# A five-stage network on one core: each stage's first row, its norm and its K and Q weights are prepared while the stage before runs its last row

## The chip, the cores and the metric

The kernel runs on 1 core of one Trainium2 chip. The metric is the device time of a run in microseconds. Everything is float32. The engines are PE (TensorE), DVE (VectorE), ACT (ScalarE), POOL (GpSimd) and SP (SyncE), which issues nearly all DMAs.

## The reference, cut to what matters

A batch of 8 rows `x[b]` of 512 tokens by 512 features goes through four layers; a "row" below is one b. The first two are linear attention: a layer norm, K, Q and V projections, a softmax of K over the tokens and of Q over the features of a head, the product of K and V, then Q times that. The third is ordinary softmax attention with 16 heads. Each of the three ends with a norm modulated by the condition `emb`, a SiLU, an output product and the residual. The fourth is a state-space layer in two directions. In the reference's terms:

```
h  = layernorm(x);  k, q, v = h @ Wk + bk, h @ Wq + bq, h @ Wv + bv
y  = attention(q, k, v, mask)
x  = x + silu(layernorm(y) * (1 + scale(emb)) + shift(emb)) @ W_out + b_out          # three times
xs = layernorm(x) * ada_scale(c) + ada_shift(c);  xn = layernorm(xs)
mx = silu(xn @ Wx.T + bx);  z = xn @ Wz.T + bz                                       # fourth layer
y  = sum over two directions of ssm(z @ Wc.T);  out = x + gate * ((y * mx) @ Wf.T + bf + xs)
```

## The kernel before, in words

`program` (L2230) runs six blocks one after the other, each closed by `sems.clear()` (L97), which frees the semaphores and ends in a barrier of all engines (L100): `prologue` (L103, modulation vectors and fused weights), `attention_layer` (L309 and on) for layer 0 and for layer 1, `softmax_layer` (layer 2), `front_layer` (the fourth layer's two norms and the products that don't depend on the scan) and `scan_layer` (the scan over time and the output). A block's SBUF tensors are its own and are given back at its end.

Within a block each engine has its own instruction list in the order in which the code issues it, and engines meet on semaphores. SP issues loads in the order written and waits in that order too.

In an attention layer a row b takes these steps: `norms(b)` on DVE (statistics L850, aggregation L854, then the normalised row `xn` L875) with the inverse root on POOL between them (L671, L673); PE transposes `xn` (stage "T", L491), ACT drains the transposes with the norm's weights into `xn_t` (L702); PE makes K (L500) and Q (L509). `norms(b + 1)` runs within row b, and so do T, K and Q of row b + 1; so only row 0 has them ahead of everything else. All engines wait for all the constants first (`const_loaded`, five DMAs). `x` has two buffers, `xn` one.

`softmax_layer` does the same with its own table: `slots` gives each step of a row (16 groups of four heads' scores) some "filler" parts of the rows around it (T, K, Q, V of the next row, YT, TY, O of the one before), which all share the bank `f_bank`. DVE's `maxima` (L1377) read the scores, ACT's exponentials and PE's transposes follow. Between them DVE has `norm_stats(b + 1)` in group 0, `normed(b + 1)` in group 1, `y_norm_stats` in group 3 and `y_normed` in group 5.

`front_layer` per row: two norms on DVE with POOL's inverse roots (statistics L1643, `xs` L1651, scale L1655, shift L1659, second statistics L1663, `xn` L1673), POOL's residual in three steps of a whole row (L1548, L1551, L1554), PE's transposes (L1590), the two small products with `w_dbc` (L1598, L1605), the 64 products with `wx` (L1615), ACT's drains. `scan_layer` begins with a product for the step size (L2017), the z product (L2035) and the fused matrices; from then on POOL's product of states (L1892) and DVE's scan (L2204) run all the time.

## Time and profile before

| | us |
|---|---|
| median of 3 runs | 5849.61 (5847.49 to 5851.81) |
| profiled execution | 5854.08 |
| its span, first to last instruction | 5852.3 |
| prologue, to the next block's first instruction | 200.8 |
| attention layer 0, attention layer 1 | 626.4, 614.1 |
| softmax layer | 1251.6 |
| front layer | 383.7 |
| scan layer | 2775.8 |

The stages are cut at each block's first POOL instruction, a memset right behind the barrier (200.81, 827.19, 1441.27, 2692.83 and 3076.54 us). The mean granted TensorE clock is 0.977 of full speed. In a timeline a line gives the start, the time from there to the end of the last of its instructions, the engine, the line of the code, the operation, the tile written and the tiles read, the count, and in brackets how long the engine had been idle and what released it. A tile's name has its block's prefix (`l_` for the attention and softmax layers, `fr_` for the front, `sc_` for the scan). SPq are DMA issues.

### The profile page before, as it was taken

The page shows a single profiled execution, that of the slowest core. Times are in us where ns is not written, and L with a number is a line of the kernel's source. Part 1 is how long each engine was busy: PE and PEld are TensorE (multiplying, and loading weights), DVE is VectorE, ACT ScalarE, POOL GpSimd, SP SyncE. Part 2 cuts the span into 40 slices and gives each one's busy share as a digit, 9 for nine tenths or more (in the row PEclk, how much of TensorE's full clock was granted, in tenths as well). Part 3 has the DMA queues.
Part 4 walks back from the last instruction along what each step waited for, and adds up shares of the span by engine and source line. Part 5 has one row for each costly group of instructions (what it writes and reads, how often), then busy time and mean ns, then how long its engine had stood idle before and what let it go on. Part 6 is the DMA issues. An engine that isn't in the chain of part 4 may idle for free. (4 is left out here: it accounts for less than half of the span.)

```text
span 5852.3 us, 136486 instructions
## 1 busy us (share of the span) xinstructions
PE 5457.4 (93%) x58510; PEld 3277.8 (56%) x58510; DVE 4269.2 (73%) x5872; ACT 2978.4 (51%) x4999; POOL 2908.6 (50%) x955
## 2 busy tenths in 40 slices
PE   8899979997898998985998999999999999999998
PEld 3455545554454555552444566666666666666665
DVE  1455535554355555565638999999999999999996
ACT  0122212221465555551116777777777777777774
POOL 0000000010000000002427999999999999999997
PEclk9999989998999999997999999999999999999999
DMA  6200020111000000002432111211111121111210
GB/s 230 73 33 32 24 77 17 36 36 49 26 1 17 17 17 17 17 8 111 155 115 84 54 62 58 67 49 46 54 60 65 58 69 54 45 49 60 65 58 32
DMA packets 145195, 321.73 MB, mean 55 GB/s; under 512 B 25945, under 2 KB 27226, under 8 KB 134378
## 3 DMA queue, kind: packets, MB, share of 16 engines
q1 hardware_dynamic: 142322, 309.20, 15.3%
q8 instruction: 448, 7.34, 0.5%
q10 hardware_dynamic: 2304, 4.20, 0.2%
q14 instruction: 121, 0.99, 0.1%
HBM read 238.46 MB, written 74.89 MB: 54 GB/s over the span
## 5 line engine op out<-in xcount | busy, mean ns | idle before, releaser
L1892 POOL TENSOR_TENSOR sc_state<-sc_state,sc_c_rows 128x2048 f32<-128x2048 f32 x512 | 2331.4, 4568 | 124.0 <-DVE sc_state L2204 123.0
L2204 DVE TENSOR_TENSOR_SCAN sc_state<-sc_decay,wide 128x512 f32<-128x512 f32 x2048 | 2335.3, 1198 | 28.0 <-PE wide L2062 20.9
L2062 PEld LDWEIGHTS wide<-sc_diag,sc_du_t 64*64 64x64 f32 x32768 | 1048.0, 133 | 526.6 <-issue 343.9
L2062 PE MATMUL wide<-sc_diag,sc_du_t 64*64 64x128 f32 x32768 | 1218.7, 272 | 19.9 <-DVE sc_state L2204 19.6
L2078 PE MATMUL wide<-sc_state,sc_half 64*64 64x512 f32 x8192 | 1199.1, 592 | 7.5 <-POOL sc_state L1892 7.0
L1996 ACT ACTIVATE sc_decay<-sc_delta,sc_neg_a 128x512 f32<-128x512 f32 x1024 | 723.6, 719 | 448.8 <-DVE sc_state L2204 443.9
L1996 ACT ACTIVATE sc_decay<-sc_delta_x,sc_neg_a 128x512 f32<-128x512 f32 x1024 | 710.0, 717 | 286.8 <-DVE sc_state L2204 282.6
L1377 DVE CUSTOM_DVE_ANT_0 l_prob<-wide,l_mask_add 128x512 f32<-128x512 f32 x512 | 340.0, 683 | 286.9 <-PE wide L1247 286.7
L2078 PEld LDWEIGHTS wide<-sc_state,sc_half 64*64 64x64 f32 x8192 | 405.6, 133 | 168.4 <-issue 127.1
L1162 ACT ACTIVATE l_prob<-l_prob,l_s_max 128x512 f32<-128x512 f32 x512 | 366.0, 716 | 229.3 <-DVE l_s_max L1377 228.9
L2035 PE MATMUL wide<-sc_xn_t,sc_w_z 128*128 128x512 f32 x1024 | 477.0, 609 | 1.7 <-DMA sc_xn_t<-xn_d 1.7
L509 PE MATMUL wide<-l_w,l_xn_t 128*128 128x512 f32 x1024 | 445.1, 592 | 1.7 <-PEq L84 1.7
L1258 PE MATMUL wide<-l_ident,l_prob 128*128 128x128 f32 x2048 | 293.2, 280 | 65.7 <-DVE l_prob_t L1386 38.5
L1258 PEld LDWEIGHTS wide<-l_ident,l_prob 128*128 128x128 f32 x2048 | 225.3, 142 | 222.5 <-issue 134.7
L1119 POOL TENSOR_TENSOR l_out<-l_x,l_rows 128x2048 f32<-128x2048 f32 x8 | 36.3, 4532 | 605.9 <-DMA x<-l_out 599.8
L509 PEld LDWEIGHTS wide<-l_w,l_xn_t 128*128 128x128 f32 x1024 | 193.1, 190 | 241.2 <-issue 241.2
L671 POOL TENSOR_SCALAR l_rstd<-l_mv 128x4 f32<-128x4 f32 x16 | 3.8, 236 | 647.5 <-DVE l_mv L854 647.5
L2035 PEld LDWEIGHTS wide<-sc_xn_t,sc_w_z 128*128 128x128 f32 x1024 | 185.3, 191 | 211.0 <-issue 211.0
L1226 PE MATMUL wide<-l_xn_t,l_w 128*128 128x512 f32 x512 | 251.0, 636 | 25.3 <-ACT l_h_t L1153 19.0
L2090 PE MATMUL wide<-sc_w_out,sc_y_sum 128*128 128x256 f32 x1024 | 244.3, 383 | 6.6 <-DVE sc_o_gated L2191 3.6
L500 PE MATMUL wide<-l_xn_t,l_w 128*128 128x512 f32 x512 | 226.2, 600 | 24.6 <-ACT l_xn_t L702 22.8
L509 PE MATMUL wide<-l_w,l_h_t 128*128 128x512 f32 x512 | 226.5, 601 | 1.7 <-ACT l_h_t L702 1.7
(203 smaller groups left out, 6669.5 us busy)
## 6 DMA issues: line engine op xcount, KB each, us to landing
sc_c_rows<-c_d SPq DMA_DIRECT2D x64, 1024.0 KB, 4.8
sc_w_z<-wz_tiles SPq DMA_DIRECT2D x128, 256.0 KB, 2.7
x<-l_out SPq DMA_DIRECT2D x24, 1024.0 KB, 4.2
l_x<-x SPq DMA_DIRECT2D x16, 1024.0 KB, 6.1
mx_d<-fr_mx SPq DMA_DIRECT2D x16, 1024.0 KB
sc_mx<-mx_d SPq DMA_DIRECT2D x64, 256.0 KB, 2.8
pro_w_mod<-in_mod_w SPq DMA_DIRECT2D x6, 2048.0 KB, 10.9
l_w<-in_att_w SPq DMA_DIRECT2D x12, 1024.0 KB, 12.5
```

The lines of the kernel that those rows point to most:

```text
L509: last = pe.matmul(bank_of(name, t)[:, :], src_t[:, k, t * P:(t + 1) * P], weight[:, k, :], start=(k == 0), stop=(k == DT - 1))
L1162: act.activation(prob[:, u % (2 * HG), :], prob[:, u % (2 * HG), :], ACT.Exp, scale=-1.0, bias=s_max[:, u % (2 * HG):u % (2 * HG) + 1], ac ...
L1226: last = pe.matmul(f_bank, weight[:, i, k * P:(k + 1) * P], xn_t[:, i, :], start=(i == 0), stop=(i == DT - 1))
L1258: last = pe.transpose(t_banks[u % 2][:, m * P:(m + 1) * P], prob[:, u % (2 * HG), m * P:(m + 1) * P], ident[:, :])
L1377: dve.tensor_tensor_reduce(out=prob[:, u % (2 * HG), :], in0=s_banks[i], in1=mask_add[b % 2][:, :], op0=ALU.add, op1=ALU.min, scale=-1.0, ...
L1892: pool.tensor_tensor(state[quad % STATES][:, :, :], state[quad % STATES][:, :, :], c_rows[(r * 4 + q) % ROWS][:, :, :], ALU.mult).then_inc ...
L1996: act.activation(decay[step % DECAYS][:, :], of[:, :], ACT.Exp, scale=neg_a[:, s, m, n:n + 1]).then_inc(decay_ready, 1)
L2035: last = pe.matmul(z_bank, w_z[slot % WZ][:, k, :], xn_t[:, k, :], start=(k == 0), stop=(k == DT - 1))
L2062: last = pe.matmul(to[cols_to, k, :, :], du_t[slot % 2][rows, k, of * 64:(of + 1) * 64], diag[r % 2][rows, c, k, :, :], start=True, stop=True)
L2078: ins = pe.matmul(acc[i][to * 64:(to + 1) * 64, :], half[g * 64:(g + 1) * 64, :], state[quad % STATES][g * 64:(g + 1) * 64, n, :], start=( ...
L2090: last = pe.matmul(z_bank[:, 0:256], y_sum[b % 2][:, k, t * P:(t + 1) * P], w_out[:, k, h * 256:(h + 1) * 256], start=(k == ks[0]), stop=( ...
L2204: dve.tensor_tensor_scan(state[quad % STATES][:, step % 4, order], decay[step % DECAYS][:, order], pair[:, i, order], 0.0, ALU.mult, ALU.a ...
```

## The change

The row buffer `x`, the norm's output `xn`, `ident` and the four weights get buffers that live across the blocks (`ahead`); the scaled row `xs` is shared from the attention layers on. In the prologue two of the three `w_mod` buffers lie over them, so the loads of row 0 and of layer 0's K and Q weights come behind the last product that reads those buffers. Every block then loads the following block's row 0 and, for the attention layers, its K and Q weights while its own last rows run, and makes the norm of that row on DVE and POOL. For the front layer, the softmax layer's last row makes both norms in six pieces, in groups 0, 1, 2, 4, 6 and 9. A block that starts counts those semaphores up instead (`sem_inc`). The wait for all constants at the head of PE and ACT goes: ACT waits for the columns alone (`cols_loaded`), which come first in SP's queue. In the front layer `w_dbc` and `wx` are loaded ahead of the ada rows and the other constants, PE waits for `w_dbc` where it uses it, and POOL's list starts with row 0's residual. In the scan layer four constants are issued on ACT's queue in place of SP's.

```diff
+                sp.wait_ge(piece_full, 4 * PIECES)
+                sp.dma_start(x[:, :, :], d["x"][0].rearrange("(t p) n -> p t n", p=P)).then_inc(x_loaded, 16)
+                for i in (1, 0):
+                    sp.dma_start(w_qk[i][:, :, :], d["att_w"][0, i].rearrange("(k p) n -> p k n", p=P)
+                                 ).then_inc(w_qk_loaded, 16)
...
@@ -363,7 +381,19 @@
...
+                dve.wait_ge(x_loaded, 16)
+                for t in range(TT):
+                    dve.bn_stats(stats[:, t, :], x[:, t, :]).then_inc(stats_ready, 1)
+                for t in range(TT):
+                    dve.wait_ge(stats_ready, t + 1)
+                    dve.bn_aggr(mv[:, t, :], stats[:, t, :]).then_inc(mv_ready, 1)
                 for j in range(2 * DT):
+                    if j == 3:
+                        dve.wait_ge(rstd_ready, 1)
+                    if 3 <= j < 3 + TT:
+                        t = j - 3
+                        dve.tensor_scalar(xn[:, t, :], x[:, t, :], mv[:, t, 0:1], rstd[:, t:t + 1],
+                                          ALU.subtract, ALU.mult)
                     dve.wait_ge(dbc_full, j + 1)
...
                     sp.sem_inc(x_stored[j], 16)
-                sp.dma_start(cols[:, :], d["att_cols"][:, layer, :]).then_inc(const_loaded, 16)
+                sp.dma_start(cols[:, :], d["att_cols"][:, layer, :]).then_inc(cols_loaded, 16)
+                sp.sem_inc(x_loaded[0], 16)
+                sp.dma_start(mask_in[0][:, :], d[f"mask{layer}"][0].broadcast_to([P, T])).then_inc(mask_loaded[0], 16)
...
-                load(0, 0)
-                for i in (1, 0, 2, 3):
+                for i in (0, 1):
+                    sp.sem_inc(w_ready[i], 16)
+                for i in (2, 3):
                     sp.dma_start(w[i][:, :, :], d["att_w"][layer, i].rearrange("(k p) n -> p k n", p=P)
                                  ).then_inc(w_ready[i], 16)
...
+                sp.wait_ge(xb_ready, B - 1)
+                sp.wait_ge(x_stored[0], 32)
+                sp.dma_start(x[0][:, :, :], x_out[0].rearrange("(t p) n -> p t n", p=P)).then_inc(x_loaded[0], 16)
+                for i, name in ((1, "K"), (0, "Q")):
+                    sp.wait_ge(psum_full, st.full(B - 2, name, 3))
+                    sp.dma_start(w[i][:, :, :], d["att_w"][layer + 1, i].rearrange("(k p) n -> p k n", p=P)
+                                 ).then_inc(w_ready[i], 16)
                 for j in range(2):
                     body(B - 2 + j, B // 2 - 1, j, False)
+                for i in range(2):
+                    sp.wait_ge(w_ready[i], 32)
...
                 def body(b, pair, j, last):
+                    norms(b + 1)
                     if not last:
-                        norms(b + 1, pair + j, 1 - j)
+                        residual(b + 1, pair + j, 1 - j)
...
-                act.wait_ge(const_loaded, 5 * 16)
+                act.wait_ge(cols_loaded, 16)
...
-                pe.wait_ge(const_loaded, 5 * 16)
...
-                dve.wait_ge(const_loaded, 5 * 16)
+                dve.sem_inc(stats_ready, TT)
+                dve.sem_inc(mv_ready, TT)
+                dve.sem_inc(xn_ready, TT)
+                dve.wait_ge(cols_loaded, 16)
+                dve.wait_ge(const_loaded, 3 * 16)
...
@@ -903,8 +949,9 @@
                 def body(b, pair, j, last):
                     if not linear:
                         mask(b, pair, j)
-                    if not last:
-                        norms(b + 1, pair + j, 1 - j)
+                    elif not last:
+                        mask(b + 1, pair + j, 1 - j)
+                    norms(b + 1, pair + j, 1 - j)
...
-                norms(0, 0, 0)
...
-                sp.dma_start(cols[:, :], d["att_cols"][:, layer, :]).then_inc(const_loaded, 16)
+                sp.dma_start(cols[:, :], d["att_cols"][:, layer, :]).then_inc(cols_loaded, 16)
+                sp.sem_inc(x_loaded, 16)
+                for i in range(2):
+                    sp.sem_inc(w_ready[i], 16)
+                sp.dma_start(w[2][:, :, :], d["att_w"][layer, 2].rearrange("(k p) n -> p k n", p=P)
+                             ).then_inc(w_ready[2], 16)
...
-                load(0)
                 load_mask(0)
-                for i in (1, 0, 2):
-                    sp.dma_start(w[i][:, :, :], d["att_w"][layer, i].rearrange("(k p) n -> p k n", p=P)
-                                 ).then_inc(w_ready[i], 16)
...
+                    if b == B - 2:
+                        sp.wait_ge(xb_ready, B)
+                        sp.wait_ge(x_stored[0], 16)
+                        sp.dma_start(x[:, :, :], x_out[0].rearrange("(t p) n -> p t n", p=P)).then_inc(x_loaded, 16)
+                        sp.dma_start(ada[:, :, :].rearrange("p r n -> p (r n)"),
+                                     d["ada_d"][0:1, 0:2 * D].broadcast_to([P, 2 * D])).then_inc(ada_loaded, 16)
...
                 for b in range(B):
-                    norms(b)
+                    if b >= 1:
+                        norms(b)
                     if b >= 2:
                         y_norms(b - 2)
                     biased(b)
+                norms(B)
                 y_norms(B - 2)
+                norms(B + 1)
...
+                def front_normed():
+                    dve.wait_ge(rstd_ready, B + 1)
+                    for t in range(TT):
+                        dve.tensor_scalar(xs[:, t, :], x[:, t, :], mv[:, t, 0:1], rstd[:, t:t + 1],
+                                          ALU.subtract, ALU.mult).then_inc(xs_normed, 1)
+
+                def front_scaled():
+                    dve.wait_ge(ada_loaded, 16)
+                    for t in range(TT):
+                        dve.wait_ge(xs_normed, t + 1)
+                        dve.tensor_tensor(xs[:, t, :], xs[:, t, :], ada[:, 0, :], ALU.mult).then_inc(xs_scaled, 1)
+
+                def front_shifted():
+                    for t in range(TT):
+                        dve.wait_ge(xs_scaled, t + 1)
+                        dve.tensor_tensor(xs[:, t, :], xs[:, t, :], ada[:, 1, :], ALU.add).then_inc(xs_ready, 1)
+
+                def front_stats():
+                    dve.wait_ge(rstd_ready, B + 1)
+                    for t in range(TT):
+                        dve.wait_ge(xs_ready, t + 1)
+                        dve.bn_stats(stats[:, t, :], xs[:, t, :]).then_inc(stats_ready, 1)
+                    for t in range(TT):
+                        dve.wait_ge(stats_ready, (B + 1) * TT + t + 1)
+                        dve.bn_aggr(mv[:, t, :], stats[:, t, :]).then_inc(mv_ready, 1)
+
+                def front_xn():
+                    dve.wait_ge(rstd_ready, B + 2)
+                    dve.wait_ge(f_full, full("T", B - 1, DT - 1))
+                    for t in range(TT):
+                        dve.tensor_scalar(xn[:, t, :], xs[:, t, :], mv[:, t, 0:1], rstd[:, t:t + 1],
+                                          ALU.subtract, ALU.mult)
...
-                    if g == 0 and b + 1 < B:
+                    if g == 0:
                         norm_stats(b + 1)
                     if g == 1 and b + 1 < B:
                         normed(b + 1)
+                    if b == B - 1:
+                        if g == 1:
+                            front_normed()
+                        if g == 2:
+                            front_scaled()
+                        if g == 4:
+                            front_shifted()
+                        if g == 6:
+                            front_stats()
+                        if g == 9:
+                            front_xn()
...
-                    sp.dma_start(x[b % 2][:, :, :], x_in[b].rearrange("(t p) n -> p t n", p=P)
-                                 ).then_inc(x_loaded[b % 2], 16)
+                    if b >= 1:
+                        sp.dma_start(x[b % 2][:, :, :], x_in[b].rearrange("(t p) n -> p t n", p=P)
+                                     ).then_inc(x_loaded[b % 2], 16)
                     sp.dma_start(ada[b % 2][:, :, :].rearrange("p r n -> p (r n)"),
                                  d["ada_d"][b:b + 1, :].broadcast_to([P, 3 * D])).then_inc(ada_loaded[b % 2], 16)
 
+                sp.sem_inc(x_loaded[0], 16)
+                sp.dma_start(w_dbc[:, :, :, :].rearrange("p s k n -> p (s k n)"), d["wdbc_d"]).then_inc(w_dbc_loaded, 16)
+                sp.dma_start(wx[:, :, :], d["wxT"].rearrange("(k p) n -> p k n", p=P)).then_inc(wx_loaded, 16)
                 load(0)
-                sp.dma_start(ident[:, :], d["ident"]).then_inc(const_loaded, 16)
                 sp.dma_start(b_bias[:, :, :].rearrange("p s n -> p (s n)"), d["dbc_bias_d"].broadcast_to([P, 192])
                              ).then_inc(const_loaded, 16)
                 for s in range(2):
...
                     if b == 0:
-                        pool.wait_ge(const_loaded, 6 * 16)
+                        pool.wait_ge(const_loaded, 4 * 16)
+                        pool.wait_ge(ada_loaded[0], 16)
...
-                for b in range(B):
+                for done in (var_ready, rstd_ready, var2_ready, rstd2_ready):
+                    pool.sem_inc(done, 1)
+                residual(0)
+                for b in range(1, B):
                     rsqrt(b, mv, rstd, mv_ready, var_ready, rstd_ready)
                     rsqrt(b, mv2, rstd2, mv2_ready, var2_ready, rstd2_ready)
                     residual(b)
...
-                act.wait_ge(const_loaded, 6 * 16)
...
-                pe.wait_ge(const_loaded, 6 * 16)
...
                     pe.wait_ge(t_drained, (b + 1) * DT)
+                    if b == 0:
+                        pe.wait_ge(w_dbc_loaded, 16)
...
+                for done in (stats_ready, mv_ready, norm_ready, scale_ready, xs_ready, stats2_ready, mv2_ready, xn_ready):
+                    dve.sem_inc(done, TT)
+                for b in range(1, B):
...
-                sp.dma_start(ident[:, :], d["ident"]).then_inc(const_loaded, 16)
...
             @block.scalar
             def _(act):
+                act.dma_start(wdt[:, :, :, :].rearrange("p s i n -> p (s i n)"), d["wdt"]).then_inc(const_loaded, 16)
+                act.dma_start(neg_a[:, :, :, :].rearrange("p s k n -> p (s k n)"), d["alog"]).then_inc(const_loaded, 16)
+                act.dma_start(ident[:, :], d["ident"]).then_inc(const_loaded, 16)
+                act.dma_start(half[:, :], d["half_ident"]).then_inc(const_loaded, 16)
...
+        with ExitStack() as shared:
+            held = lambda n, s: shared.enter_context(nc.sbuf_tensor("ahead_" + n, s, F32))
+            pairs = [held("xn_wq", [P, ET, 512]), held("x_wk", [P, ET, 512])]
+            ahead = {"ident": held("ident", [P, P]), "xn": pairs[0][:, 0:TT, :], "x": pairs[1][:, 0:TT, :],
+                     "w": [p[:, TT:ET, :] for p in pairs], "w_mod": pairs}
+            prologue(nc, sems, d, mod_all, banks, ahead)
+            sems.clear()
+            ahead["w"] += [held("w2", [P, DT, D]), held("w3", [P, DT, D])]
+            ahead["xs"] = held("xs", [P, TT, D])
```

The first place where instructions move is DVE in the softmax layer's last row, at group 2. `l_prob` are the scores with the mask, `l_prob_t` the transposed probabilities, `l_y` the rescaled attention output of the row before. Before:

```order
L1386 COPY l_prob_t<-wide 128x512
L1377 ISA l_prob,l_s_max<-wide,l_mask_add 128x512
L1377 ISA l_s_max 128x1
L1352 TENSOR_TENSOR l_y<-wide,l_q_sum 128x512 x2
L1377 ISA l_prob,l_s_max<-wide,l_mask_add 128x512
L1377 ISA l_s_max 128x1
```

And after the change, where `ahead_xs` is the front layer's scaled row:

```order
L1478 COPY l_prob_t<-wide 128x512
L1469 ISA l_prob,l_s_max<-wide,l_mask_add 128x512
L1469 ISA l_s_max 128x1
L1444 TENSOR_TENSOR l_y<-wide,l_q_sum 128x512
L1397 TENSOR_TENSOR ahead_xs<-ahead_xs,l_ada 128x512 x4
L1444 TENSOR_TENSOR l_y<-wide,l_q_sum 128x512
L1469 ISA l_prob,l_s_max<-wide,l_mask_add 128x512
```

A multiplication of four instructions now stands between the two drains of `l_y`; five other pieces stand in groups 0, 1, 4, 6 and 9.

The second is POOL's list at the start of the front layer, up to row 1's second inverse root (`fr_rstd`), before:

```order
L1532 MEMSET fr_minus_half 128x4
L1537 TENSOR_SCALAR fr_rstd<-fr_mv 128x4
L1539 TENSOR_TENSOR fr_rstd<-fr_rstd,fr_minus_half 128x4
L1537 TENSOR_SCALAR fr_rstd<-fr_mv 128x4
L1539 TENSOR_TENSOR fr_rstd<-fr_rstd,fr_minus_half 128x4
L1548 TENSOR_TENSOR fr_resid<-fr_xs,fr_bf_row 128x2048
L1551 TENSOR_TENSOR fr_resid<-fr_resid,fr_ada 128x2048
L1554 TENSOR_TENSOR fr_resid<-fr_resid,fr_x 128x2048
L1537 TENSOR_SCALAR fr_rstd<-fr_mv 128x4
```

And after:

```order
L1634 MEMSET fr_minus_half 128x4
L1651 TENSOR_TENSOR fr_resid<-ahead_xs,fr_bf_row 128x2048
L1654 TENSOR_TENSOR fr_resid<-fr_resid,fr_ada 128x2048
L1657 TENSOR_TENSOR fr_resid<-fr_resid,ahead_x_wk 128x2048
L1639 TENSOR_SCALAR fr_rstd<-fr_mv 128x4
L1641 TENSOR_TENSOR fr_rstd<-fr_rstd,fr_minus_half 128x4
L1639 TENSOR_SCALAR fr_rstd<-fr_mv 128x4
L1641 TENSOR_TENSOR fr_rstd<-fr_rstd,fr_minus_half 128x4
```

Row 0's two inverse roots are gone from it, and the three steps of row 0's residual stand ahead of row 1's inverse roots.

The third is SP's list at the same place, before:

```order
L1487 DMA fr_x<-x 128x4x512
L1489 DMA fr_ada<-ada_d 128x1536
L1493 DMA fr_ident<-in_ident 128x128
L1494 DMA fr_b_bias<-dbc_bias_d 128x192
L1497 DMA fr_c_bias<-dbc_bias_d 80x1 x2
L1499 DMA fr_bf_row<-in_bf_row 128x512
L1500 DMA fr_w_dbc<-wdbc_d 128x768
L1502 DMA fr_wx<-in_wxT 128x4x1024
L1487 DMA fr_x<-x 128x4x512
```

And after:

```order
L1596 DMA fr_w_dbc<-wdbc_d 128x768
L1597 DMA fr_wx<-in_wxT 128x4x1024
L1592 DMA fr_ada<-ada_d 128x1536
L1599 DMA fr_b_bias<-dbc_bias_d 128x192
L1602 DMA fr_c_bias<-dbc_bias_d 80x1 x2
L1604 DMA fr_bf_row<-in_bf_row 128x512
L1590 DMA fr_x<-x 128x4x512
L1592 DMA fr_ada<-ada_d 128x1536
```

The two weights went to the head, row 0 is no longer loaded, and row 1 and its ada rows stay behind the small constants.

## Rows read from the trace of the kernel before

**Rows 1.** Page, part 1: busy us, share, instructions of PE.

```profile
PE 5457.4 (93%) x58510; PEld 3277.8 (56%) x58510; DVE 4269.2 (73%) x5872; ACT 2978.4 (51%) x4999; POOL 2908.6 (50%) x955
```

**Rows 2.** Timeline, first attention start: start, us, engine, line, op, tiles, count, [idle, releaser].

```profile
200.81 0.10 POOL L663 MEMSET l_minus_half<- 128x4 f32 x1 [197.35 <-POOLq L100]
...
206.40 0.18 DVE L842 TENSOR_SCALAR l_keep<-l_keep_in 128x32 f32<-128x32 int32 x1 [7.80 <-DMA l_keep_in<-in_mask_t]
...
218.86 3.34 ACT L702 ACTIVATE l_xn_t<-wide,l_cols 128x512 f32<-128x512 f32 x4 [43.84 <-PE wide L491]
...
222.25 14.00 PE L500 MATMUL wide<-l_xn_t,l_w 128*128 128x512 f32 x32 [0.87 <-ACTq L84]
```

**Rows 3.** Timeline, second attention start.

```profile
827.19 0.10 POOL L663 MEMSET l_minus_half<- 128x4 f32 x1 [29.33 <-POOLq L100]
...
848.40 16.24 PE L500 MATMUL wide<-l_xn_t,l_w 128*128 128x512 f32 x32 [0.87 <-ACTq L84]
```

**Rows 4.** Timeline, softmax stage start.

```profile
1441.27 0.10 POOL L1105 MEMSET l_minus_half<- 128x4 f32 x1 [28.66 <-POOLq L100]
...
1461.22 0.78 ACT L1147 ACTIVATE l_xn_t<-wide,l_cols 128x512 f32<-128x512 f32 x1 [1.21 <-PE wide L1215]
...
1466.03 6.03 PE L1226 MATMUL wide<-l_xn_t,l_w 128*128 128x512 f32 x8 [0.87 <-ACT l_xn_t L1147]
```

**Rows 5.** DMA issues: tiles, kind, count, KB, median us to landing.

```profile
ssm_cols<-in_ssm_cols SPq DMA_DIRECT2D x1, 36.0 KB, 1.8
```

**Rows 6.** Timelines of POOL, DVE and PE, front stage, first two rows.

```profile
2692.83 0.10 POOL L1532 MEMSET fr_minus_half<- 128x4 f32 x1 [35.77 <-POOLq L100]
...
2715.45 4.49 POOL L1548 TENSOR_TENSOR fr_resid<-fr_xs,fr_bf_row 128x2048 f32<-128x2048 f32 x1
...
2700.34 2.47 DVE L1643 BATCH_NORM_STATS2 fr_stats<-fr_x 128x6 f32<-128x512 f32 x4 [12.80 <-DMA fr_ada<-ada_d]
...
2715.51 14.44 DVE L1673 TENSOR_SCALAR fr_xn<-fr_xs,fr_mv,fr_rstd 128x512 f32<-128x512 f32 x4 [1.47 <-POOL fr_rstd L1539]
...
2734.08 1.91 DVE L1651 TENSOR_SCALAR fr_xs<-fr_x,fr_mv,fr_rstd 128x512 f32<-128x512 f32 x4 [1.47 <-POOL fr_rstd L1539]
...
2745.65 13.78 DVE L1673 TENSOR_SCALAR fr_xn<-fr_xs,fr_mv,fr_rstd 128x512 f32<-128x512 f32 x4
...
2734.82 7.09 PE L1598 MATMUL wide<-fr_xn_t,fr_w_dbc 128*80 128x512 f32 x16 [0.87 <-ACT fr_xn_t L1570]
...
2772.79 1.04 PE L1590 MATMUL wide<-fr_ident,fr_xn 128*128 128x128 f32 x8
```

**Rows 7.** Timeline of DVE, softmax stage, rows 6 and 7 of eight.

```profile
2391.67 0.69 DVE L1377 CUSTOM_DVE_ANT_0 l_prob<-wide,l_mask_add 128x512 f32<-128x512 f32 x1 [0.25 <-PE wide L1247]
...
2395.31 2.47 DVE L1315 BATCH_NORM_STATS2 l_stats<-l_x 128x6 f32<-128x512 f32 x4
...
2398.55 0.68 DVE L1377 CUSTOM_DVE_ANT_0 l_prob<-wide,l_mask_add 128x512 f32<-128x512 f32 x1
...
2405.21 0.68 DVE L1377 CUSTOM_DVE_ANT_0 l_prob<-wide,l_mask_add 128x512 f32<-128x512 f32 x1
...
2539.98 0.69 DVE L1377 CUSTOM_DVE_ANT_0 l_prob<-wide,l_mask_add 128x512 f32<-128x512 f32 x1 [0.25 <-PE wide L1247]
...
2544.96 0.69 DVE L1377 CUSTOM_DVE_ANT_0 l_prob<-wide,l_mask_add 128x512 f32<-128x512 f32 x1 [0.65 <-PE wide L1247]
...
2551.09 0.69 DVE L1377 CUSTOM_DVE_ANT_0 l_prob<-wide,l_mask_add 128x512 f32<-128x512 f32 x1 [0.36 <-PE wide L1247]
```

**Rows 8.** Timeline, scan stage start.

```profile
3078.35 0.48 SPq L1756 DMA_DIRECT2D sc_dlt<-dlt_d  x1
...
3087.25 6.07 PE L2035 MATMUL wide<-sc_xn_t,sc_w_z 128*128 128x512 f32 x8 [1.68 <-DMA sc_xn_t<-xn_d]
```

**Rows 9.** Timeline, first attention layer, last row.

```profile
768.61 0.18 DVE L910 RECIPROCAL l_k_sum<-l_k_sum 128x4 f32<-128x4 f32 x1
...
781.30 1.91 PE L491 MATMUL wide<-l_ident,l_k_t 128*128 128x128 f32 x16
```

106 lines of the change are left out of this document (56 added, 50 removed).

## The prediction

> **What bounds the kernel now.** I read the page's busy times first, then timelines around each of the five places where one stage ends and the next begins, then the softmax stage's last two rows of the batch. PE is busy for 93% of the span [rows 1], so little is to be had inside the stages; the reader is to look at their starts. There PE stands idle. R below is the moment when a stage's first POOL instruction, a memset, runs, right behind the barrier.
>
> In the first attention stage R is 200.81 and the first K product starts at 222.25, which is R + 21.4. Between them the constants land (DVE L842 at 206.40 is released by the last of them), then row 0, then its norm runs, then the transposes and ACT's four drains of 3.34 us [rows 2]. In the second it is 848.40 - 827.19 = 21.2 [rows 3], in the softmax stage 1466.03 - 1441.27 = 24.8 [rows 4]. The front stage is the dearest: its first product is at 2734.82, R + 42.0, because row 0 goes through two norms and because DVE's last normalisation takes 14.44 us beside POOL's residual, which starts at the same moment (2715.45 against 2715.51) [rows 6]. The scan stage starts its z product when xn_t has landed [rows 8].
>
> **Part by part.** (1) Attention starts. Loading row 0, its statistics, rsqrt and normalisation leave the start; K and Q weights are there already. PE's first 16 transposes can run at once, since PE waits for no constant any more. What is late next is ACT's first drain, which needs the column constants, the first DMA of SP. A transfer of like kind landed 1.8 us after its issue [rows 5], so with the issue at R + 0.1 ACT drains from R + 2.2, needs its 3.34 us [rows 2], and K starts at R + 5.6. Gain 21.4 - 5.6 = 15.8 and 21.2 - 5.6 = 15.6. DVE still waits for all constants (R + 5.6 before [rows 2]) and the mask, but K's first group comes only some 3.5 us after K starts (a fourth of 14.00 [rows 2]), at R + 9, so this wait is covered; if the mask came after that, each us would cost one. Bounds: if ACT's constants came only when all five did before, R + 5.6, K would start at R + 9.0 and each gain be 3.4 smaller; the other end is the clock.
>
> (2) The clock. In the second stage the first matmuls ran at the lower level, 1.2 GHz: 32 products took 16.24 us, against 14.00 in the first stage [rows 2, 3], so a start at the lower level costs 2.2. The second stage keeps its cost. The first one ran its K at full clock after the transposes; I allow 0.5 there for a later rise, and take 15.3; the ends are 0 and 2.2. The Trainium skill (TensorE: Matmul & The Clock Gate, section "What's actually happening") says that the throttled state is the default and activity releases it; by that every start, the first one too, pays the full amount, and the first gain would be 13.6 instead of 15.3.
>
> (3) Softmax start. Its transposes go through a single bank: each step is a drain of 0.78 and a wait of 1.21 [rows 4]. With the first drain at R + 2.3 the fourth ends at R + 2.3 + 3 x 1.99 + 0.78 = R + 9.05, and K follows at R + 9.1. Gain 24.8 - 9.1 = 15.7; its first 8 products keep their 6.03 us. Bounds 12.3 (constants late by 3.4) and 17.9 (clock up in time).
>
> (4) Front start. PE starts its transposes at R + 0.2 and w_dbc is now SP's first load, so row 0's products start at about R + 5 instead of R + 42. By that alone the gain would be 37. But row 1 is late next. Before, DVE had row 1's xn ready long before PE asked (DVE's 13.78 us from 2745.65 end at 2759.4, PE's transposes start at 2772.79 [rows 6]). Now POOL has row 0's residual in its queue ahead of row 1's rsqrt, and it waits for the constants and the ada rows. These stand behind 2.5 MB of weights in SP's queue: about 3.6 MB in all. Before, 1.8 MB were in at R + 7.5 (DVE L1643 at 2700.34 [rows 6]); with 2 us before the first byte that is 0.33 MB per us, so I estimate 2 + 3.6 / 0.33 = R + 13. POOL's three steps at 4.49 end at R + 26.5; rsqrt and its hand-over take 1.5; DVE starts xs of row 1 at R + 28, comes to xn 11.6 later (2734.08 to 2745.65) at R + 39.6, and needs 13.8 there beside POOL's next residual: R + 53.4. PE, going from R + 5 by the old distance of 38.0 (2734.82 to 2772.79), asks at R + 43. It stalls for 10.4 us. Row 1's transposes come at R + 53.4 instead of R + 80.0: gain 26.6, less 1 which I allow for matmuls at the lower clock after that stall, 25.7. Row 2 has time to spare again, because a DVE row (about 30 us: 2.8 of statistics, 1.5, 11.6 and 13.8) is shorter than PE's 42. Bounds: 37 without the stall, 22 if POOL starts 4 us later still.
>
> (5) Scan start. Four DMA issues ahead of SP's other loads go to ACT's queue, about 0.45 us each by their neighbour [rows 8], so at most 1.8. The z product waits for xn_t, whose bytes still share the engines with these constants; I take 1.3, between 0 and 2.5. The Trainium skill (DMA: Bandwidth & Descriptors, section "Queues, rings and completion order") says that a DMA engine takes turns between queues packet by packet; by that the constants no longer stand ahead of xn_t but beside it, the same bytes come first, and the gain would be near 0 instead of 1.3.
>
> (6) What is added. Where a last row runs, DVE now does the next stage's row. In the two attention stages that is a norm of about 6.5 us right behind 768.61, which every other row has too; k_t is then ready at about 777, and PE asks for it at 781.30 [rows 9]. Covered, cost 0; without the cover 6.5 each. In the prologue DVE mostly waits for PE; 0. The softmax stage's last row is not free: DVE's new blocks stand between the maxima that PE's scores wait for. How dear such a block is, rows 6 and 7 tell. With the statistics (2.47 and 0.36) the step from 2391.67 to 2398.55 takes 6.88, the same step without them 4.98 (2539.98 to 2544.96): 1.90. With the normalisation of 1.9 us the next one takes 6.66 against 6.13: 0.53 [rows 7]. The last row gets six blocks: statistics 1.9, normalisation 0.5, scale 1.35, shift 1.65 (each 2.4 us long, so between the two), second statistics 1.5, second normalisation 0.1 to 0.3 beside output products. Together 7.0 lost. Bounds: 4 (all at the cheaper price per us of block) and 14 (all six exposed).
>
> **Sum.** 15.3 + 15.6 + 15.7 + 25.7 + 1.3 - 7.0 = 66.6 us. The profiled execution took 5854.1 (span 5852.3), so 5787.5 by its own measure; it lies 4.5 above the median of the runs, 5849.6, and for a median I forecast 5783.
>
> **Rivals.** A: the front stall doesn't come, since DVE's xn slips between POOL's steps or POOL starts early. The order of the rows is against it: POOL and DVE started together and DVE lost 12.5 us [rows 6]. Then 10.4 + 1 us more: 5772. B: the starts stay bound by constants, at R + 5.6 as before, in all three attention-like stages, and w_dbc comes late by 2: 3 x 3.4 = 10.2 less, 5793. For it: SP issues one DMA after another; against it: the columns are first. C, slower than before: POOL's long instructions hold DVE's normalisations wherever they are put. There are 20 added or moved ones (4 in the prologue, 4 in each attention stage, 8 in the softmax stage). One held takes (14.44 - 0.5) / 3 = 4.6 instead of about 0.5 [rows 6], 4.1 more; 20 x 4.1 = 82, and with nothing of it covered the sum turns to 15 slower, 5865. It decides from 17 of 20 held. Against it: POOL is idle in those last rows. D: the change doesn't bring the work forward, because a preload lands late and DVE, which runs in order, stops in front of it with the maxima behind it. The start's gain of one stage (15) is then spent where it was won, twice over if both: 5799 to 5815.
>
> **Chances.** The forecast 0.66, A 0.12, B 0.12, D 0.06, C 0.04. All bounds together at the good end give 15.8 + 17.8 + 17.9 + 37 + 2.5 - 4 = 87, at the bad end 11.9 + 12.2 + 12.3 + 22 + 0 - 14 = 44, so 5763 to 5805. They won't all fall one way; 5769 to 5800 holds A and B and leaves about 2 in 10 out. A measurement of this kernel can tell about 0.2%, 12 us, from no change: faster 0.94, within it 0.02, slower 0.04.
>
> **What would show it.** Right: K products at R + 5 to 6 in the attention stages and R + 9 in the softmax stage; PE idle for 8 to 12 us ahead of row 1's transposes in the front stage, with POOL's residual ahead of row 1's rsqrt; the last softmax row longer by 5 to 9 us. Wrong: K waits that end with a DMA of constants, a DVE wait for a preload in a last row, normalisations of 4.7 us in last rows, or a longer scan stage.

## The result and the profile after

| | before | after |
|---|---|---|
| median of the runs, us | 5850.71 (5847.49 to 5852.04, 4 runs) | 5797.5 (5793.07 to 5798.61, 4 runs) |
| ratio to the kernel before | | 0.9908 (95%: 0.9891 to 0.9926) |
| profiled execution, its span | 5854.08, 5852.3 | 5797.34, 5795.2 |
| prologue | 200.8 | 199.3 |
| attention layer 0, attention layer 1 | 626.4, 614.1 | 617.4, 602.0 |
| softmax layer | 1251.6 | 1237.7 |
| front layer | 383.7 | 362.6 |
| scan layer | 2775.8 | 2776.2 |

The kernel is 53 us faster, where 66.6 were forecast (5783); the time lies near the upper end of the range given (5769 to 5800). Between the two profiled executions the spans differ by 57.1: 1.5 + 9.0 + 12.1 + 13.9 + 21.1 - 0.5, block by block. These are two single executions, and a block of the same code differs by 2 to 7 us from one profile to the next; the table in "Why the prediction came out as it did" has the spread. R, the moment of a block's first POOL memset, is 199.34, 816.72, 1418.70, 2656.37 and 3018.99 now. The line of part 1 of the page that answers to [rows 1] has the same work in a shorter span:

```profile
PE 5459.9 (94%) x58510; PEld 3280.3 (57%) x58510; DVE 4264.0 (74%) x5872; ACT 2978.3 (51%) x4999; POOL 2907.3 (50%) x956
```

The start of the first attention layer after the change, a timeline (against [rows 2]):

```profile
199.34 0.10 POOL L703 MEMSET l_minus_half<- 128x4 f32 x1 [20.48 <-POOLq L100]
...
207.11 0.18 DVE L890 TENSOR_SCALAR l_keep<-l_keep_in 128x32 f32<-128x32 int32 x1 [10.12 <-DMA l_keep_in<-in_mask_t]
207.34 4.53 POOL L722 TENSOR_TENSOR l_out<-ahead_x_wk,l_rows 128x2048 f32<-128x2048 f32 x1 [7.91 <-DMA l_keep_in<-in_mask_t]
207.44 4.71 DVE L908 TENSOR_SCALAR l_mask_add<-l_mask_in 128x512 f32<-128x512 int32 x1
207.50 3.65 PE L520 MATMUL wide<-ahead_ident,ahead_xn_wq 128*128 128x128 f32 x16 [10.89 <-DVEq L84]
208.62 3.34 ACT L747 ACTIVATE l_xn_t<-wide,l_cols 128x512 f32<-128x512 f32 x4 [33.58 <-PE wide L520]
212.01 15.95 PE L529 MATMUL wide<-l_xn_t,ahead_x_wk 128*128 128x512 f32 x32 [0.87 <-ACTq L84]
```

The row at 207.50 is the one to look at. Row 0's `xn` had been finished at 191.1, PE waited for no constant in its own list, and yet its transposes start at R + 8.2. The bracket says what released them: DVE's sequencer at L84, a semaphore count, right behind the instruction at 207.11 that a DMA of constants released. L84 is `absent`: each engine counts up the drains that row 0 doesn't have, and PE's first transposes wait for DVE's count. It stands behind DVE's wait for the constants, as it did before, where `xn` came later anyway. K starts at R + 12.7, not R + 5.6. The second attention layer (against [rows 3]) shows the same, with K at R + 11.4:

```profile
823.73 3.50 PE L520 MATMUL wide<-ahead_ident,ahead_xn_wq 128*128 128x128 f32 x16 [13.29 <-DVEq L84]
...
828.10 14.00 PE L529 MATMUL wide<-l_xn_t,ahead_x_wk 128*128 128x512 f32 x32 [0.87 <-ACTq L84]
```

The softmax layer counts nothing of the kind, and its start (against [rows 4]) went as forecast, K at R + 8.5:

```profile
1420.43 0.78 ACT L1204 ACTIVATE l_xn_t<-wide,l_cols 128x512 f32<-128x512 f32 x1 [23.92 <-DMA l_cols<-in_att_cols]
...
1427.22 5.61 PE L1282 MATMUL wide<-l_xn_t,ahead_x_wk 128*128 128x512 f32 x8 [0.87 <-ACT l_xn_t L1204]
```

The front layer's first two rows after the change, timelines of POOL, DVE and PE (against [rows 6]):

```profile
2671.61 4.51 POOL L1651 TENSOR_TENSOR fr_resid<-ahead_xs,fr_bf_row 128x2048 f32<-128x2048 f32 x1 [15.13 <-DMA fr_bf_row<-in_bf_row]
...
2697.46 4.51 POOL L1651 TENSOR_TENSOR fr_resid<-fr_xs,fr_bf_row 128x2048 f32<-128x2048 f32 x1
...
2676.97 2.47 DVE L1751 BATCH_NORM_STATS2 fr_stats<-fr_x 128x6 f32<-128x512 f32 x4 [25.93 <-DMA fr_ada<-ada_d]
...
2686.66 1.91 DVE L1759 TENSOR_SCALAR fr_xs<-fr_x,fr_mv,fr_rstd 128x512 f32<-128x512 f32 x4 [6.95 <-POOL fr_rstd L1641]
...
2697.52 14.46 DVE L1781 TENSOR_SCALAR fr_xn<-fr_xs,fr_mv,fr_rstd 128x512 f32<-128x512 f32 x4
...
2661.94 9.46 PE L1704 MATMUL wide<-fr_xn_t,fr_w_dbc 128*80 128x512 f32 x16 [0.87 <-ACT fr_xn_t L1675]
...
2712.03 3.96 PE L1694 MATMUL wide<-ahead_ident,fr_xn 128*128 128x128 f32 x16 [9.60 <-DVE fr_xn L1781]
...
2716.86 9.30 PE L1704 MATMUL wide<-fr_xn_t,fr_w_dbc 128*80 128x512 f32 x16 [0.87 <-ACT fr_xn_t L1675]
```

This is the stall that the prediction worked out: POOL's residual of row 0 waits for the constants, row 1's inverse root waits for the residual, row 1's `xn` then takes 14.46 us beside the next residual, and PE stands for 9.60 us ahead of row 1's transposes. These come at R + 55.7 instead of R + 80.0.

In the softmax layer's last row (against [rows 7]) DVE's maxima of groups 1, 2 and 3 start here; between them stand the statistics and the two normalisations:

```profile
2496.59 0.69 DVE L1469 CUSTOM_DVE_ANT_0 l_prob<-wide,l_mask_add 128x512 f32<-128x512 f32 x1 [0.25 <-PE wide L1303]
...
2500.23 2.47 DVE L1374 BATCH_NORM_STATS2 l_stats<-ahead_x_wk 128x6 f32<-128x512 f32 x4
...
2503.47 0.68 DVE L1469 CUSTOM_DVE_ANT_0 l_prob<-wide,l_mask_add 128x512 f32<-128x512 f32 x1
...
2507.71 1.90 DVE L1390 TENSOR_SCALAR ahead_xs<-ahead_x_wk,l_mv,l_rstd 128x512 f32<-128x512 f32 x4
...
2510.13 0.68 DVE L1469 CUSTOM_DVE_ANT_0 l_prob<-wide,l_mask_add 128x512 f32<-128x512 f32 x1
```

The first step is 6.88 us (4.98 before, [rows 7]), the second 6.66 (6.13 before). Each maxima row that starts a group gives one such step. Against the same steps before, the six blocks cost 1.90, 0.53, 1.11 (scale), 1.67 (shift), 1.33 (second statistics) and 0.24 (`xn`): 6.8. The first five repeat within 0.02 us in the five other profiles of this code; the last doesn't (that step takes 8.16 to 8.88 us in them, against 8.55 before), so 0.24 is inside the spread. The normalisations in all the last rows took 1.90 to 1.92 us for four, so POOL held none of them.

In the last row of the first attention layer (against [rows 9]) DVE's norm stands ahead of the same reciprocal, `k_t` is ready at 768.4, and PE asks for it at 772.98. It cost nothing: from the last K product's start to the end of the layer it is 100.5 us, against 102.7 before (102.2 to 102.3 in four of the five other profiles of the same code, 100.5 in one), and in the second attention layer 102.1 us before and after.

```profile
764.66 1.92 DVE L921 TENSOR_SCALAR ahead_xn_wq<-ahead_x_wk,l_mv,l_rstd 128x512 f32<-128x512 f32 x4 [1.58 <-POOL l_rstd L715]
766.49 0.17 DVE L957 RECIPROCAL l_k_sum<-l_k_sum 128x4 f32<-128x4 f32 x1
...
772.98 1.91 PE L520 MATMUL wide<-ahead_ident,l_k_t 128*128 128x128 f32 x16
```

### The profile page after: what moved, and what is told of

Read it like the earlier page. It is cut to its first block and busy times, and to the rows that moved or that the text cites. A ratio compares the mean times of both kernels' runs of the same rounds, so it can differ in the third digit from the quotient of the medians.

```text
span 5795.2 us, 136527 instructions
## 1 busy us (share of the span) xinstructions
PE 5459.9 (94%) x58510; PEld 3280.3 (57%) x58510; DVE 4264.0 (74%) x5872; ACT 2978.3 (51%) x4999; POOL 2907.3 (50%) x956
## 3 DMA queue, kind: packets, MB, share of 16 engines
q10 hardware_dynamic: 2880, 4.95, 0.2%
## 5 line engine op out<-in xcount | busy, mean ns | idle before, releaser
L1314 PE MATMUL wide<-ahead_ident,l_prob 128*128 128x128 f32 x2048 | 294.1, 281 | 66.8 <-DVE l_prob_t L1478 39.2
L1314 PEld LDWEIGHTS wide<-ahead_ident,l_prob 128*128 128x128 f32 x2048 | 227.3, 143 | 224.0 <-issue 133.8
L1173 POOL TENSOR_TENSOR l_out<-ahead_x_wk,l_rows 128x2048 f32<-128x2048 f32 x8 | 36.3, 4535 | 610.1 <-DMA x<-l_out 598.4
L529 PE MATMUL wide<-l_xn_t,ahead_x_wk 128*128 128x512 f32 x512 | 225.9, 599 | 24.6 <-ACT l_xn_t L747 22.8
L747 ACT ACTIVATE l_k_tm<-wide 128x512 f32<-128x512 f32 x64 | 33.1, 607 | 379.4 <-PE wide L520 379.4
L1721 PE MATMUL wide<-fr_xn_t,fr_wx 128*128 128x512 f32 x512 | 226.8, 604 | 0.0
L538 PE MATMUL wide<-ahead_w,l_h_t 128*128 128x512 f32 x512 | 224.4, 597 | 1.7 <-ACT l_h_t L747 1.7
L538 PE MATMUL wide<-ahead_w,l_xn_t 128*128 128x512 f32 x512 | 222.5, 593 | 1.0 <-PEq L84 1.0
```

The lines of the kernel that those rows point to most:

```text
L538: last = pe.matmul(bank_of(name, t)[:, :], src_t[:, k, t * P:(t + 1) * P], weight[:, k, :], start=(k == 0), stop=(k == DT - 1))
L1314: last = pe.transpose(t_banks[u % 2][:, m * P:(m + 1) * P], prob[:, u % (2 * HG), m * P:(m + 1) * P], ident[:, :])
L1721: last = pe.matmul(banks[6 + m % 2], wx[:, k, m * P:(m + 1) * P], xn_t[j][:, k, :], start=(k == 0), stop=(k == DT - 1))
```

## The experiments

In each, times are medians against the kernel before on the same chip, with its ratio and 95% interval. The block lengths are from the profiled execution. The changed kernel's ratio, 0.9908, has the interval 0.9891 to 0.9926, and most of the intervals below overlap it. So what one edit did is read from the timelines, and the medians only agree with it; of the edited versions of the changed kernel, the last one alone is clear of it by its interval.

### DVE's count ahead of its waits

```diff
                 dve.sem_inc(xn_ready, TT)
+                first = [i[0] for i in plan].index("T")
+                absent(st, dve, drained["dve"], "dve", -1, plan[0][0], first)
                 dve.wait_ge(cols_loaded, 16)
...
-                first = [i[0] for i in plan].index("T")
-                absent(st, dve, drained["dve"], "dve", -1, plan[0][0], first)
```

> The changed kernel with one edit in both attention stages: DVE counts its absent parts up before it waits for the constants, not behind. In the changed kernel PE's transposes of row 0 started at R + 8.2 and R + 7.0, released by that count, and K at R + 12.7 and R + 11.4. My theory (PE waits for DVE's count, which stands behind the constants): the transposes start at R + 0.3, K at about R + 5.6 in both, 7.1 and 5.8 us earlier; K at the lower clock may take back 2 in the second. Time 5785 to 5788 against 5797.5 of the changed kernel, ratio to the kernel before 0.989. Rival (the transposes or ACT's drains are late by the DMAs themselves): K stays between R + 10 and R + 13, time 5796 to 5799, ratio 0.991.

Measured: 5782.26 us, ratio 0.9885 (0.9869 to 0.9902). The attention layers last 611.8 and 595.9 us instead of 617.4 and 602.0. Their start in PE's and ACT's timelines, with R at 201.12:

```profile
201.69 3.65 PE L520 MATMUL wide<-ahead_ident,ahead_xn_wq 128*128 128x128 f32 x16 [3.29 <-DVEq L84]
206.20 16.21 PE L529 MATMUL wide<-l_xn_t,ahead_x_wk 128*128 128x512 f32 x32 [0.87 <-ACTq L84]
...
202.92 3.23 ACT L747 ACTIVATE l_xn_t<-wide,l_cols 128x512 f32<-128x512 f32 x4 [26.08 <-DMA l_cols<-in_att_cols]
```

The transposes start at R + 0.6 and K at R + 5.1 (R + 5.5 in the second layer); ACT's first drain is at R + 1.8, released by the column constants, as the prediction had it. So the step was right in all but the one count that it overlooked. K runs at the lower clock in both layers (16.21 and 15.60 us for 32 products). The two blocks together are 11.7 us shorter than in the changed kernel's own profile, in which the second K ran at the higher clock. Against the five other profiles of the same attention code they are 13.4 to 16.1 us shorter, and the medians differ by 15.2.

### PE's own wait put back

```diff
             def _(pe):
+                pe.wait_ge(cols_loaded, 16)
+                pe.wait_ge(const_loaded, 3 * 16)
```

> The changed kernel, with PE in the two attention stages waiting again for the columns and the three other constants before anything else. My theory (PE is held by DVE's count, which comes behind the same constants, so its own wait was worth nothing): K at R + 12.7 and R + 11.4 within 0.3, time 5797.5 within 2, ratio 0.991. Rival (dropping PE's own wait is what gave the gain at the starts): K 3 to 6 us later in each, time 5803 to 5809, ratio 0.992 to 0.993.

Measured: 5795.29 us, ratio 0.9907 (0.989 to 0.9923), beside 0.9908 of the changed kernel. K at R + 12.8 and R + 11.7. The two layers last 619.7 and 604.1 us, which is 2.3 and 2.1 more than in the changed kernel's profile, but the same as in the fifth and sixth experiment (619.7 and 604.1; 619.4 and 604.1), which leave these layers alone. PE's wait could be given back at no cost, since DVE's count held it just as long: in the changed kernel its removal was worth nothing.

### The residual behind `xn`

```diff
                     pool.wait_ge(xs_ready, (b + 1) * TT)
+                    pool.wait_ge(xn_ready, (b + 1) * TT)
```

> The changed kernel, with POOL's residual of every front row waiting also until DVE has written that row's xn. In the changed kernel row 1's xn took 14.46 us beside the residual and PE stood 9.6 us before row 1's transposes (R + 55.7), with a lower clock behind it. My theory (the two hold each other): xn of row 1 takes about 1.9 us and ends near R + 43, PE starts the transposes at R + 46 without a stall, 9.6 us earlier, and 0 to 2.8 of clock come back. Time 5785 to 5788, ratio 0.989. Rival (the later residual delays the loads and xs of the rows behind): PE stalls by 5 us or more before row 2 or 3, time 5793 to 5800.

Measured: 5783.57 us, ratio 0.9883 (0.9867 to 0.99), the front layer 349.6 us instead of 362.6. Timelines of DVE and PE, with R at 2659.21:

```profile
2700.27 1.91 DVE L1782 TENSOR_SCALAR fr_xn<-fr_xs,fr_mv,fr_rstd 128x512 f32<-128x512 f32 x4
...
2705.09 1.04 PE L1695 MATMUL wide<-ahead_ident,fr_xn 128*128 128x128 f32 x8
```

The same four instructions take 1.91 us instead of 14.46, and the transposes start at R + 45.9 without a wait. The rows behind are not late: DVE's `xs` of row 2 starts at R + 58.1, in the changed kernel at R + 59.7. Three other profiles have the changed kernel's front code (first, second and sixth experiment): there row 1's transposes come at R + 54.8 to R + 54.9 and the block lasts 359.4 to 359.5 us. Against these the gain is 9.0 at the transposes and 9.8 in the block.

### Row 1's inverse roots ahead of the residual

```diff
-                residual(0)
                 for b in range(1, B):
                     rsqrt(b, mv, rstd, mv_ready, var_ready, rstd_ready)
                     rsqrt(b, mv2, rstd2, mv2_ready, var2_ready, rstd2_ready)
+                    if b == 1:
+                        residual(0)
                     residual(b)
```

> The changed kernel, with row 1's two inverse roots ahead of row 0's residual in POOL's list. By my prediction's step (row 1 is late because its inverse root stands behind the residual in POOL's queue) DVE's xs of row 1 starts at R + 25 instead of R + 30.3, its xn at about R + 36, and since POOL then starts row 0's residual at the same moment, xn still takes 14.4 us: transposes of row 1 at R + 50.2 instead of R + 55.7, stall 4 us instead of 9.6, time 5791 to 5794, perhaps 1 to 3 worse by a late row 2 because two residuals follow each other. Rival (POOL's order is not what sets row 1, the late load is): xs of row 1 stays at R + 30, time 5797.

Measured: 5792.25 us, ratio 0.9902 (0.9886 to 0.9919), the front layer 356.3 us. Timelines of POOL and PE, with R at 2656.99:

```profile
2679.50 0.24 POOL L1639 TENSOR_SCALAR fr_rstd<-fr_mv 128x4 f32<-128x4 f32 x1 [22.41 <-DVE fr_mv L1755]
...
2691.70 4.52 POOL L1651 TENSOR_TENSOR fr_resid<-ahead_xs,fr_bf_row 128x2048 f32<-128x2048 f32 x1
...
2706.31 1.10 PE L1695 MATMUL wide<-ahead_ident,fr_xn 128*128 128x128 f32 x8 [3.27 <-DVE fr_xn L1782]
```

`xs` of row 1 starts at R + 23.9 and the transposes at R + 49.3, with a wait of 3.3 us. POOL's order was worth 6.3 us (5.5 to 5.6 against the three other profiles); the rest is the collision, which this order keeps (`xn` 14.49 us).

### `wx` behind row 1

```diff
                 sp.dma_start(w_dbc[:, :, :, :].rearrange("p s k n -> p (s k n)"), d["wdbc_d"]).then_inc(w_dbc_loaded, 16)
-                sp.dma_start(wx[:, :, :], d["wxT"].rearrange("(k p) n -> p k n", p=P)).then_inc(wx_loaded, 16)
                 load(0)
...
                 load(1)
+                sp.dma_start(wx[:, :, :], d["wxT"].rearrange("(k p) n -> p k n", p=P)).then_inc(wx_loaded, 16)
```

> The changed kernel, with the 2 MB of wx behind row 1 and its ada rows in SP's queue of the front stage, not ahead of them. In the changed kernel POOL's residual of row 0 started at R + 15.2, DVE's statistics of row 1 at R + 20.6, xs at R + 30.3 and PE's transposes of row 1 at R + 55.7. My prediction's step (the weights ahead hold up the constants, and with them the residual and row 1): residual at R + 9, xs of row 1 at R + 24, its xn at R + 35 and still 14.4 us long beside the next residual, transposes at R + 49.5, 6 us earlier; the wx products wait up to 2 us for wx. Time 5790 to 5793. Rival (the constants land when they do because of their own small transfers, not the weights): residual at R + 14 or later, transposes at R + 54 or later, time 5796 to 5799.

Measured: 5783.76 us, ratio 0.9888 (0.9873 to 0.9903), the front layer 352.7 us. POOL's and DVE's timelines, with R at 2655.39:

```profile
2664.00 4.50 POOL L1651 TENSOR_TENSOR fr_resid<-ahead_xs,fr_bf_row 128x2048 f32<-128x2048 f32 x1 [8.51 <-DMA fr_bf_row<-in_bf_row]
...
2668.53 2.47 DVE L1751 BATCH_NORM_STATS2 fr_stats<-fr_x 128x6 f32<-128x512 f32 x4 [18.49 <-DMA fr_ada<-ada_d]
```

The residual starts at R + 8.6 instead of R + 15.2 and the transposes of row 1 at R + 49.1 instead of R + 55.7: 6.6 us (5.8 to 5.9 against the three other profiles). The 2 MB ahead were the reason. The block gains 9.9, because row 1's `w_dbc` products ran at full clock (7.09 us instead of 9.30); against the three other profiles, where they did too, it gains 6.7. The median is lower than forecast; its softmax layer lasted 1230.7 us, 7 less than in the changed kernel, at an edit that doesn't touch it.

### The front's row 0 in the tail of the softmax layer

```diff
-                    if g == 0:
+                    if g == 0 and b + 1 < B:
                         norm_stats(b + 1)
...
-                    if b == B - 1:
-                        if g == 1:
-                            front_normed()
...
                 y_normed(B - 1)
+                norm_stats(B)
+                front_normed()
+                front_scaled()
+                front_shifted()
+                front_stats()
                 for k in range(4):
                     drain("O", B - 1, k)
+                    if k == 0:
+                        front_xn()
...
-                norms(B)
                 y_norms(B - 2)
-                norms(B + 1)
                 y_norms(B - 1)
+                norms(B)
+                norms(B + 1)
```

> The changed kernel, with DVE's six blocks for the front layer's row 0 moved from the groups of the softmax stage's last row to its tail, behind the last normalised y and between the output drains, where DVE stood idle for 14.6 us and then 3.8 us at a time. In the changed kernel the stretch from the last K product's start to the end of that stage was 275.1 us against 267.9 before, at the same time of low clock (37.5 and 37.7 us). My theory (the blocks stand between the maxima that PE's scores wait for, and cost 7): 267.9 within 1 at a like clock, time 5789 to 5792. Rival (the 7 us come from something else in that row, or the tail pays them back): 274 to 276, time 5796 to 5799.

Measured: 5790.74 us, ratio 0.9898 (0.9882 to 0.9913). The stretch from the last K product's start to the block's end, as windows (length; PE, PEld, DVE, ACT, POOL busy; granted clock; DMA share; GB/s), first in the kernel before, then in the changed kernel, then in this one:

```profile
2424.97:2692.83 267.86, 220.14 (x1764) 124.17 (x1760) 135.57 (x323) 139.73 (x297) 7.08 (x5) 0.93 0.03 13
```

```profile
2381.30:2656.37 275.07, 221.45 (x1764) 125.00 (x1760) 148.47 (x355) 139.74 (x297) 9.58 (x9) 0.93 0.05 18
```

```profile
2386.00:2652.51 266.51, 217.29 (x1764) 122.63 (x1760) 149.41 (x355) 139.66 (x297) 9.59 (x10) 0.95 0.05 19
```

At the same clock the change made it 7.2 longer, with DVE's 32 instructions more; here DVE has them too, and the stretch is 266.5 at a slightly higher clock (27.3 us at the lower level instead of 37.4, which is worth some of it). The first six steps between the maxima behind group 1 are those of before (4.98, 6.13, 6.13, 6.31, 4.95, 5.47). DVE's timeline shows where the blocks went:

```profile
2618.43 2.46 DVE L1374 BATCH_NORM_STATS2 l_stats<-ahead_x_wk 128x6 f32<-128x512 f32 x4
...
2629.29 2.46 DVE L1408 BATCH_NORM_STATS2 l_stats<-ahead_xs 128x6 f32<-128x512 f32 x4
...
2633.02 0.69 DVE L1456 TENSOR_TENSOR l_out<-wide,l_out 128x512 f32<-128x512 f32 x1 [0.99 <-PE wide L1289]
```

DVE had just become free when the first output product needed draining; it still waited 0.99 us for PE.

### The kernel before with the residual behind `xn`

The edit is the one line of the third experiment, made in the kernel before.

> The kernel before, with one edit: POOL's residual of a front row waits until DVE has written the row's xn. My theory (DVE's xn of row 0 takes 14.44 us only because the residual starts beside it): that xn takes 1.9 us, the front stage's first product starts 12.5 us earlier, at R + 29.5 instead of R + 42.0, and the later residual costs nothing; the kernel gets 12.5 faster, 5838, ratio 0.9979. So about a third of what the change gains at the front start would be had without preparing anything. Rival (row 1 is late instead, as in the changed kernel): PE stalls ahead of row 1's transposes and 5845 to 5850 remain.

Measured: 5841.07 us, ratio 0.9982 (0.9973 to 0.9991). `xn` of row 0 takes 1.91 us and the first product starts at R + 29.6 (2719.20 - 2689.65), 12.4 us earlier; the block is 10.2 shorter, since the 16 `w_dbc` products now run partly at the lower clock (9.31 us instead of 7.09). So of the 42 us that the front layer's start took, 12 were this collision.

The edit doesn't touch the softmax layer, so this run is also a second profile of that layer as it was before:

```profile
2419.98:2689.65 269.67, 219.33 (x1764) 123.56 (x1760) 135.36 (x323) 139.81 (x297) 7.07 (x6) 0.93 0.03 13
```

The last stretch takes 269.67 us here and 267.86 in the kernel before, at the same clock and with the same instructions. So this stretch is known to about 2 us, and the 7.2 that the change cost there is 5.4 against this profile.

### The four mends together

The edits of the first, third and sixth experiment, and the scan layer's four constants on SP's queue as in the kernel before.

> The changed kernel with four edits together: DVE's count of absent parts ahead of its waits in the attention stages, the front's residual behind xn, the front's preparation in the softmax stage's tail, and the scan's four constants back on SP's queue. If the parts add up: 15 + 14 + 7 + 0.5 less than the changed kernel's 5797.5, so 5759 to 5764, ratio to the kernel before 0.985. Rival (they share a cause, or the clock takes part of it back): 5768 or more.

Measured: 5767.28 us (5764.0 to 5770.91), ratio 0.9861 (0.9846 to 0.9876). It is the fastest kernel here, 30 us under the changed one, though a little above the band forecast and below the rival's. The blocks are 611.8, 595.9, 1228.9, 349.5 and 2776.7 us, against 617.4, 602.0, 1237.7, 362.6 and 2776.2. K starts at R + 5.1 and R + 5.6, row 1's transposes at R + 45.8. The last stretch of the softmax layer is 1.9 us longer than in the kernel before's own profile, at the same clock:

```profile
2366.07:2635.80 269.73, 219.35 (x1764) 123.62 (x1760) 149.35 (x355) 139.80 (x297) 9.60 (x9) 0.93 0.05 19
```

That is not a loss of this mend. One step between maxima, from group 11 to 12, is 11.24 us here and 10.14 in the sixth experiment; but it is 11.26 in the seventh, with the old softmax code, and 10.15 in the kernel before. The stretch as a whole is 269.73 here and 269.67 in the seventh, so with the mend it is as long as before, at a like clock. What decides that step is open.

## Why the prediction came out as it did

**Where the time was to come from** was right in the main: the starts of the blocks (the scan's excepted), and nothing inside them but the softmax layer's last row. By its own steps, in us:

| step | forecast | measured |
|---|---|---|
| first attention start | +15.3 | +6.8: K 8.8 earlier, and 1.95 lost at the lower clock |
| second attention start | +15.6 | +12.1: K 9.8 earlier, and 2.2 won at the higher clock, by luck (below) |
| softmax start | +15.7 | +16.2 |
| front start | +25.7 | +24.3 at row 1's transposes, +21.1 at the end |
| scan start | +1.3 | -0.5 |
| softmax last row | -7.0 | -7.2 |
| prologue, rest | 0 | 1.5 + 2.2 + 4.9 |
| sum | 66.6 | 57.1 |

**The step that failed** is the sentence "PE's first 16 transposes can run at once, since PE waits for no constant any more". PE's list was read for waits on constants, and not for what its other waits stand on. The count at L84 sits in DVE's list behind `const_loaded`, and the constants themselves landed later than before (R + 7.8 instead of R + 5.6; the mask now stands ahead of them in the queue, but whether that is why was not tried). That is 7.1 and 5.8 us; the first experiment gave them back, and the second showed that taking out PE's own wait had been worth nothing. Rival B had a like mechanism, constants that hold the starts, but priced it at 3.4 in each of three stages; it was 7.1 and 5.8 in two, and nothing in the softmax layer. Its time, 5793, is nearer to the measured 5797.5 than the forecast's 5783, so the range held although this step failed.

**The clock at the attention starts** was under-priced. The prediction allowed 0.5 at the first start and left the second as it was. There are eight profiles of the changed attention starts, two starts each: 32 K products took 15.6 to 16.4 us in fourteen of them and 14.00 in two (the changed kernel's second start and the third experiment's first). So the first start pays about 2 as well, which is the other reading that the prediction gave (13.6 instead of 15.3), and the 2.2 won at the second start is luck of the one profile.

**The front** went as worked out: residual from R + 15.2 (forecast R + 13), `xn` of row 1 at R + 41.2 (R + 39.6) for 14.46 us (13.8), stall 9.6 (10.4). Two errors offset each other in the stall: row 1 was ready 2 us later than forecast, and PE asked at R + 46.1 instead of R + 43, since row 0's `w_dbc` products now ran partly at the lower clock (9.46 us instead of 7.09). Each link was tested alone: the queue order (6.3), the 2 MB ahead (6.6), the collision (9.8). They don't add up, since the stall that they share is 9.6. Rival A fell with it. The loss of 3.2 us from there to the next row was allowed at 1: row 1's `w_dbc` products took 9.30 us at 0.75 of the clock. In the three other profiles of the same front code they took 7.09, and the loss is 0.8: the block's gain is there 24.2 to 24.3 instead of 21.1, against 25.7 forecast.

**The softmax last row** was priced block by block from two rows of before, and all six blocks came within 0.25 us of it. The sixth and the eighth experiment show that it need not be paid at all: the forecast accepted the place of the blocks and didn't ask where DVE stood idle.

**The scan start** was mis-sized. In the seven profiles with the constants on ACT's queue the z product starts between R + 9.7 and R + 11.2 (middle 10.0), in the three with SP's queue between R + 10.4 and R + 11.0 (10.7). The blocks last 2773.7 to 2777.0 and 2775.8 to 2776.7. So some 0.7 us may be there, and it is lost in the spread. The Trainium skill (DMA: Bandwidth & Descriptors, section "Queues, rings and completion order"), by which queues share an engine packet by packet, would have said about 0, and that is nearer than 1.3.

**What no step had** are the 8.6 us of the last line but one, and much of that is the spread of single profiles. The blocks of the changed kernel, beside the experiments that leave the block's code as it is:

| block | changed kernel's profile | others of the same code |
|---|---|---|
| prologue | 199.3 | 199.2 to 201.6 (7) |
| attention layer 0 | 617.4 | 617.0 to 619.7 (5) |
| attention layer 1 | 602.0 | 604.1 to 605.2 (5) |
| softmax layer | 1237.7 | 1230.7 to 1237.5 (5) |
| front layer | 362.6 | 359.4 to 359.5 (3) |
| scan layer | 2776.2 | 2773.7 to 2777.0 (6) |

The prologue's 1.5 is inside it (the two profiles of the old prologue have 200.8 and 201.3). In the softmax layer, from the K products of row 2 to those of row 7, five rows, it is 745.5 us in the kernel before and 740.6 in the changed one, with the same instructions. In the experiments that leave that layer alone, the third of these rows lasts 146.9 to 147.0 us in four kernels, where no time in it has the lower granted clock, and 149.9 in one, with 10.2 us at the lower clock (149.9 in the kernel before, also with 10.2). A single profile can therefore not tell 5 us there. So part of the 57.1 is luck, in both directions (2 too much in attention layer 1, 3 too little in the front layer), and so is part of how near the sum comes to the forecast; the median gained 53. Rivals C and D didn't come: no normalisation in a last row was held, and no wait in a last row ended with a preload.

## What to carry to other kernels

When a wait is removed to start an engine earlier, list every semaphore that the engine's first instruction waits for. For each, look up in the list of the engine that increments it what stands ahead of the increment; the release shown in brackets in the profile names it once the dearer wait is gone. Work that is prepared ahead belongs where the engine is seen idle in the timeline (here 14 us in the tail), not where a slot of the loop happens to be. When the first of several rows gets earlier, forecast the second with the same care: its queue order, its loads and its collisions set the gain.
